# The two key halves of a row's maximum in neighbouring PSUM banks, taken by one VectorE instruction

## The reference, cut to what matters

```python
scores = jnp.einsum('bhdn,bhdm->bhnm', q, k) * scale
attn = jax.nn.softmax(scores, axis=-1)
out = jnp.einsum('bhnm,bhdm->bhdn', attn, v)
```

## Time and profile before

| | us |
|---|---|
| three runs | 578.43, 582.92, 582.92 |
| median | 582.92 |
| span of the profiled execution | 580.5 |
| PE busy | 507.5 (87%), 2731 matmuls |
| DVE busy | 356.6 (61%), 654 instructions |
| ACT busy | 292.6 (50%), 520 instructions |

### The profile page before, as it was taken

How to read it: one execution, slowest core, us unless ns; L and a number is a source line. 1 busy time by engine, 2 the same in 40 slices (tenths; PEclk the granted TensorE clock), 3 DMA queues, 4 the chain that set the end, 5 groups by cost and what they waited for, 6 DMA issues and landing times.

```text
span 580.5 us, 7014 instructions
## 1 busy us (share of the span) xinstructions
PE 507.5 (87%) x2731; PEld 221.8 (38%) x2731; DVE 356.6 (61%) x654; ACT 292.6 (50%) x520; POOL 10.5 (2%) x13
## 2 busy tenths in 40 slices
PE   7757899988997999878997999889999999899884
PEld 2411222232242564222242554212244553467574
DVE  2569869688669562488669562487463644743324
ACT  2400575664752463564752563547776573244352
POOL 7000000000000000000000000000000000000000
PEclk9955799998998899998998999989999999999998
DMA  8682000026000000026000000000000000000003
GB/s 292 128 171 45 2 1 1 1 53 112 0 2 1 2 0 1 1 54 110 0 3 1 2 0 0 2 0 1 1 3 0 1 0 0 2 1 1 1 1 73
DMA packets 7473, 15.52 MB, mean 27 GB/s; under 512 B 1424, under 2 KB 4496, under 8 KB 7184
## 3 DMA queue, kind: packets, MB, share of 16 engines
q1 hardware_dynamic: 7440, 15.07, 11.6%
HBM read 10.77 MB, written 4.19 MB: 26 GB/s over the span
## 4 chain that ended last, share of the span: by engine, by line
PE 62%; DVE 24%; ACT 7%; DMA 4%; issue 2%; SPq 1%; ACTq 0%; DVEq 0%
DVE part_max L1006 11%; PE O L624 8%; PE S L611 5%; PE M L592 5%; PE R L678 4%; PE R L750 4%; PE R L760 4%; PE R L731 4%; PE R L746 3%; PE R L553 2%; PE R L561 2%; DVE zs L1090 2%; DMA KX<-qk_scratch 2%; DVE neg_m L1095 2%; ACT probs L884 1%
## 5 line engine op out<-in xcount | busy, mean ns | idle before, releaser
L884 ACT ACTIVATE probs<-S 128x512 f32<-128x512 f32 x219 | 124.4, 595 | 137.2 <-PE S L611 136.5
L1006 DVE TENSOR_REDUCE part_max<-M 128x1 f32<-128x512 f32 x208 | 135.0, 684 | 37.8 <-PE M L592 37.5
L592 PE MATMUL M<-KX,QX 96*128 96x512 bf16 x208 | 82.7, 417 | 25.0 <-DVE part_max L1006 15.5
L611 PE MATMUL S<-QX,KX 99*128 99x512 bf16 x219 | 83.7, 396 | 6.6 <-ACT probs L884 4.6
L624 PE MATMUL O<-probs,VT 128*32 128x512 f32 x512 | 70.4, 624 | 1.5 <-ACT probs L884 1.4
L592 PEld LDWEIGHTS M<-KX,QX 96*128 96x128 bf16 x208 | 20.5, 99 | 76.3 <-DVE part_max L1006 54.6
L611 PEld LDWEIGHTS S<-QX,KX 99*128 99x128 bf16 x219 | 21.3, 99 | 66.9 <-issue 32.0
L1129 DVE TENSOR_TENSOR zs<-R,rden 128x512 f32<-128x512 f32 x32 | 22.1, 689 | 25.1 <-ACT rden L917 25.0
L1121 DVE TENSOR_TENSOR p<-p,s_rest 128x512 f32<-128x512 f32 x32 | 22.0, 688 | 23.9 <-ACT p L908 23.7
L750 PE MATMUL R<-p,x_tok 128*128 128x256 f32 x128 | 33.1, 381 | 0.8 <-DVE zs L1129 0.6
L731 PE MATMUL R<-z,xbd 128*128 128x256 f32 x96 | 30.3, 409 | 1.2 <-ACT p L908 1.2
(11 more groups left out here) (213 smaller groups left out, 685.5 us busy)
## 6 DMA issues: line engine op xcount, KB each, us to landing
qk_scratch<-qk_part SPq DMA_DIRECT2D x8, 384.0 KB, 4.6
zs<-early SPq DMA_DIRECT2D x1, 2048.0 KB, 8.1
QX<-qk_scratch SPq DMA_DIRECT2D x4, 384.0 KB, 5.1
KX<-qk_scratch SPq DMA_DIRECT2D x4, 384.0 KB, 6.9
s_rest<-rest SPq DMA_DIRECT2D x1, 1042.0 KB, 11.3
QX<-qk_scratch SPq DMA_DIRECT2D x4, 256.0 KB, 7.7
KX<-qk_scratch SPq DMA_DIRECT2D x4, 256.0 KB, 8.4
result<-probs SPq DMA_DIRECT2D x2, 512.0 KB, 5.2
```

The costliest lines, as they stand in the source:

```text
L592: mm(max_ring(n)[n % ring], QX[b % 2][0:KQ, half, h, nt * P:(nt + 1) * P], KX[b % 2][0:KQ, kh, h, :], start=True, stop=True).then_inc(g["m ...
L611: mm(ring[n % len(ring)], KX[b % 2][:, j // QT, h, j % QT * P:(j % QT + 1) * P], QX[b % 2][:, half, h, :], start=True, stop=True).then_inc ...
L884: A(probs[:, u % 2, h, :], ring[(H0 * n + h) % len(ring)], ACT.Exp, scale=HD ** -0.5).then_inc(g["exp_done"], 1)
L1006: nc.vector.tensor_reduce(part_max[:, row, kh:kh + 1], max_ring(n)[n % len(max_ring(n))], AX_X, ALU.max).then_inc(g["max_red"], 1)
```

## The change

One reduction takes both pieces of a row. `part_max` has one column a row instead of two. DVE does nothing at a piece with kh = 0; at kh = 1 it reduces 128 x 2 x 512 elements, two neighbouring banks, over both axes into that column (`max_pair`). `max_red` so counts rows, not pieces. PE waits only ahead of a piece with kh = 0, and then for the row that used that pair of banks before: two rows ago with two pairs (M and S in half 0, M and R1, R2 in halves 1 and 2), one row ago with the single pair M from half 3 on. `max_neg` has no two columns to join and negates with a multiplication by -1. Banks, matmuls, their number and the order of stages stay.

```diff
-        part_max = sb("part_max", [P, ROWS, 2])
+        part_max = sb("part_max", [P, ROWS])
...
+        def max_pair(n):
+
+            pairs = [M[:, 0:2, :]] + ([S[:, 0:2, :]] if n < PIECES else [R[:, 1:3, :]] if n < 3 * PIECES else [])
+            return pairs[n // 2 % len(pairs)]
...
-                ring = len(max_ring(n))
-                if n >= ring:
-                    pe.wait_ge(g["max_red"], n - ring + 1)
-                mm(max_ring(n)[n % ring], QX[b % 2][0:KQ, half, h, nt * P:(nt + 1) * P], KX[b % 2][0:KQ, kh, h, :],
+                pairs = len(max_ring(n)) // 2
+                if kh == 0 and n // 2 >= pairs:
+                    pe.wait_ge(g["max_red"], n // 2 - pairs + 1)
+                mm(max_ring(n)[n % (2 * pairs)], QX[b % 2][0:KQ, half, h, nt * P:(nt + 1) * P], KX[b % 2][0:KQ, kh, h, :],
                    start=True, stop=True).then_inc(g["max_mm"], 1)
...
             def max_piece(b, half, i):
                 row, kh = divmod(i, 2)
                 n = (2 * b + half) * PIECES + i
+                if kh == 0:
+                    return
                 dve.wait_ge(g["max_mm"], n + 1)
-                nc.vector.tensor_reduce(part_max[:, row, kh:kh + 1], max_ring(n)[n % len(max_ring(n))], AX_X, ALU.max).then_inc(g["max_red"], 1)
+                nc.vector.tensor_reduce(part_max[:, row:row + 1], max_pair(n), mybir.AxisListType.XY, ALU.max).then_inc(g["max_red"], 1)
 
             def max_neg(b, half):
-                dve.wait_ge(g["max_red"], (2 * b + half + 1) * PIECES)
+                dve.wait_ge(g["max_red"], (2 * b + half + 1) * ROWS)
                 for p in range(PARTS):
-                    last = nc.vector.tensor_reduce(neg_max[:, p, :], part_max[:, :, :], AX_X, ALU.max, negate=True)
+                    last = nc.vector.tensor_scalar(neg_max[:, p, :], part_max[:, :], -1.0, None, ALU.mult)
                 last.then_inc(g["negmax"], 1)
```

## The result

| | before | after |
|---|---|---|
| median of four runs, us | 582.77 (578.43 to 582.92) | 631.38 (630.72 to 633.09) |
| ratio to before | | 1.0855 [1.0817, 1.0893] |
| span of the profiled execution, us | 580.5 | 631.3 |
| mean granted clock of TensorE | 0.947 | 0.908 |

The change makes the kernel 8.6% slower. I had forecast slower, but 612.5 us and at most 627. The medians lie 48.6 us apart and the two profiled executions, which the text takes apart from here on, 50.8 us in span; I had 29.6.

What follows compares the result with a forecast made beforehand. DVE bounds half 0 and most of half 2, PE half 1; from half 3 on both wait in turn. Span 580.5 + 2.4 around it + 29.6 over halves 0 to 7 = 612.5 us, range 598 to 627.

Steps and rivals of the forecast that it cites:

- the hold of a pair: From a row's second piece to the next first piece on the same banks: 0.42 + 1.21 + 0.05 = 1.68 us.
- DVE's saving: Over all 128 double reductions, 0.07 us saved on each: 9 us of DVE's 357.
- the stall from half 3 on: PE's added waiting with one pair of banks: halves 3 to 7 grow by 5.6, 4.5, 5.6, 4.5 and 5.8 us.
- 0.6 back at `fc1`: Half 5, likewise half 3: `fc1` waits for a layer norm today and then no longer does, -0.6 us.
- 0.5 at `fc2`: Half 5, likewise half 3: the pair's delay is covered by `fc2`, -0.5 us.
- the one bare gap in the block stage: Halves 4 and 6: one A-to-B gap a half, 1.46 us, half of it absorbed, +0.6 us.
- the 15 steps of half 5: Delays between the 16 pairs of half 5, worked out from starts of pieces and reductions; sum 5.6 us.
- rival (1): TensorE's clock falls in five to ten more places, +6 to +20 us; chance 0.22, shared with a dearer reduction.
- signs of being wrong: Double reduction well under 1.1 us, PE's new gaps replacing existing waits for ACT, or the clock's row changing much.
- (2): Other PE waits absorb the stalls: half, 595 to 600 us, chance 0.14; nearly all, within 1%, chance 0.06.
- (3): Halves 0 to 7: DVE's throughput is the bound wherever line 1006 is on the chain; 574 us, chance 0.03.
- (4): Reading across two banks costs 1.37 us, at about 55 exposed gaps +9, 621 us; chance 0.22, shared with clock falls.

Runs made afterwards that it cites:

- the two filled kernels: The kernel before (583.10 us, ratio 1.0028) and the changed kernel (617.21 us, ratio 1.0618), each with unread matmuls added where TensorE waits.
- the filled change: The changed kernel with unread matmuls ahead of kh = 0 pieces at 34 places from half 3 on: 617.21 us, ratio 1.0618.

## Why the prediction was right in sign and wrong in size

*Right.* The price of the new reduction (1.21, measured 1.22), the hold of a pair (1.68, measured 1.70; 2.08 behind a layer norm, measured 2.08), its place (second piece to next first piece), the release of the second pieces, and that DVE's saving is worth nothing from half 3 on. (The hold's sum took 0.05 us for the release where its own row gave 0.06; it makes no difference.) Halves 0, 1 and 2: forecast 0, 2.1 and 1.5 us; measured, as the growth from each half's first piece to the next half's first, 0, 2.3 and 1.3. Rows of these stretches were DVE-bound or PE-bound before, and the two-pair ring cost what had been worked out, within 0.2 us a half. The small misses of halves 1 and 2 cancel each other, which is luck.

*Mis-sized: the stall from half 3 on.* The sum had 26.0 us, and 3.6 in front. First to last piece, in the two filled kernels, the clock at 1.00 but where the table says otherwise:

| half | before, us | change, us | growth | forecast |
|---|---|---|---|---|
| 3 | 40.3 | 47.1 | 6.8 | 5.6 |
| 4 | 50.6 | 56.7 | 6.1 | 4.5 |
| 5 | 40.6 | 47.4 | 6.8 | 5.6 |
| 6 (before has 3.4 at half clock) | 51.4 | 56.7 | 5.3 | 4.5 |
| 7 (3.4 at half clock in both) | 35.8 | 41.9 | 6.1 | 5.8 |

31.1 for 26.0. Three of my credits failed. In halves 3 and 5 I gave 0.6 back at `fc1` and 0.5 at `fc2`, on the ground that those matmuls wait for other engines and would not wait any more; measured, these gaps are as long as before (2.57 and 2.55 us; 3.63 and 3.62), so what they wait for came later by as much. That is 1.1 of the 1.2 us. In halves 4 and 6 I halved the one bare gap in the block stage, saying that its chain of exponential, mask, sum and reciprocal would absorb the rest (+0.6); measured in the filled change it is 2.1 us longer, 2.29 in place of 0.22, and those 1.5 us are nearly all that half 4 grew beyond the forecast (1.6). At these three places a stall of TensorE moved the chain that I had expected to absorb it. Elsewhere the walk held: of the 15 steps of half 5 the other 13 came within 0.2 us of the forecast, those covered by `den` and `o_norm` among them (-0.01, -0.06 and -0.23 us, forecast 0, -0.1 and -0.2).

*The step that failed: the clock was left out of the sum.* The sum added only stalls, as if TensorE's clock stayed as before; the runs show some 17 us that go with 55 us more at half clock. I had it as rival (1), 618 to 632 us, in a case with the chance 0.22, on the mechanism that came true: seven more falls, for the five to ten that it named, and 631.4 us, at its upper end. It belonged into the forecast. The earlier trace rows already showed a fall after a stretch in which PE had been busy for 4.06 of 6.70 us, and my own arithmetic left a plain unit 3.3 us of issue in 6.0. Against this I set an average of 75% over a half. The average was right and said nothing: the stretch of half 5 after the change has PE busy for 39.31 of 53.00 us, 74%, and the clock at 0.84; even before, with 36.90 of 44.00, it had a fall (0.96). A falling clock's row was also among the signs of being wrong that I had named. One fall of the changed kernel and the stretch ahead of it:

```profile
188.00:191.40 3.40, 1.90 (x68) 0.90 (x67) 3.28 (x8) 1.19 (x2) 0.00 (x0) 1.00 0.02 5
191.40:198.20 6.80, 5.75 (x62) 1.56 (x62) 6.08 (x8) 1.20 (x2) 0.00 (x0) 0.50 0.00 1
```

PE busy for 1.90 of 3.40 us at clock 1.00, then 6.8 us at 0.50. The price in that rival (1.1 to 2.3 us for a fall of 3.4 to 6.8, that is 0.33 us a us) was close to the 0.3 that the difference of the filled kernels gives; what I had wrong was its chance, and so the forecast. In all: 3.6 us in halves 0 to 2 as forecast, 31 of stalls for 26, and 17 with the clock where the sum had none.

The rivals (2), (3) and (4) fell: less was absorbed than I had allowed, not more; DVE is no bound once the pair is single (it stands idle 71.3 us for the matmuls into M); and two banks in one instruction cost no more than their elements. The advice that I weighed (the Trainium skill, Perfetto Trace Analysis, "Optimizing Scalar/DVE Operations": break instructions up where the engine isn't saturated but causes bubbles on another) agrees with this case, though its mechanism needs naming: reducing in two instructions at the same late moment is worse (1.1029) than one (1.0855), starting the first one early but holding the pair is better (1.0618), and giving each bank back by itself, as the kernel before does, is best. The 125 ns of overhead on PSUM that the Trainium skill states in the same section isn't what a back-to-back reduction gave up here: the pair of them takes 1.28 us, the single one 1.22.

## What to carry to other kernels

Before merging two reductions, ask who waits for the banks. Count the hold, from the last write into them to their release, against the producer's other work at each place; if the ring shrinks to one, the reduction stands bare wherever that work is shorter, and the few per cent of VectorE time saved don't enter. Then, if the trace before has falls of TensorE's clock at all, price the producer's new gaps twice: once as waiting, once as more time at the lower clock (0.2 to 0.4 us for each us at half speed in the runs here), and look at short stretches for it, not at the average of a stage. Don't credit other engines' waits with absorbing a stall of the engine that feeds them, unless the trace shows that they wait for something else.

## What the runs showed of the hardware that I had not expected

- TensorE's stalls came with a second price, half as large as the first: 34 us of waiting and, by difference, 17 us that go with 55 us more at the lower of its two clock levels (0.5 of full, 1.2 GHz).
- Raising the clock in the kernel before brought nothing measurable (17 us less at half clock, ratio 1.0028 [0.9994, 1.0061]), while in the changed kernel the same means brought 2.2% (1.0855 to 1.0618). Single halves gained 0.26 us a us in the kernel before (halves 3 and 5); why the whole kernel before doesn't show it stays open. The fillers' own cost is one suspect. The other is that a fall has no fixed price: in the run with pairs in halves 0 to 2 alone, half 4 took 51.0 us with 10.2 us at half speed, and in the kernel before, with the same waits and reductions there, 51.9 us with 6.8.
- One more 0.06 us of hold a pair (two reductions in place of one, both late) came out as 12 us, with 28 us more at half clock. If those cost 0.3 us each, they are 8 of the 12; this is an estimate from the figures above, not a measurement.
